# Attention stage of a macaron transformer layer: other steps for the scaling, the turns and the norms

## What is computed

```python
x = x + 0.5 * ffn(layernorm(x))
x = x + attn(layernorm(x), W_q, W_k, W_v, W_o)
x = x + 0.5 * ffn(layernorm(x))

def attn(x, W_q, W_k, W_v, W_o):          # 16 heads of 16
    q, k, v = (proj(W) for W in (W_q, W_k, W_v))
    scores = where(causal, q @ k.T / 4, -65504.0)
    return (softmax(scores) @ v).reshape(b, s, d) @ W_o.T
```

## Time and profile before

| | us |
|---|---|
| median of the three executions | 1705.95 |
| the profiled execution's own time | 1703.97 |
| its span, from first to last instruction | 1702.0 |
| TensorE busy | 1552.6 (91%) |
| VectorE, ScalarE, POOL busy | 886.3, 583.8, 590.4 |
| mean granted TensorE clock | 0.956 of full speed |

### The profile page before, as it was taken

How to read it: one execution, slowest core, us unless ns; L and a number is a source line. 1 busy time by engine, 2 the same in 40 slices (tenths; PEclk the granted TensorE clock), 3 DMA queues, 4 the chain that set the end, 5 groups by cost and what they waited for, 6 DMA issues and landing times. The chain is left out here.

```text
span 1702.0 us, 27697 instructions
## 1 busy us (share of the span) xinstructions
PE 1552.6 (91%) x8388; PEld 1138.9 (67%) x8389; DVE 886.3 (52%) x1844; ACT 583.8 (34%) x1110; POOL 590.4 (35%) x832
## 2 busy tenths in 40 slices
PE   6699999999999948989998999856999999999998
PEld 5688885666668835556665666535888766666787
DVE  5377633333336637666565666515775333333466
ACT  1322222222223224545554555514222222222232
POOL 3328812333330043453454353422377033333200
PEclk9999999999999978999998999867999999999999
DMA  7678832222237334344444344124196322222661
GB/s 235 212 268 286 288 122 76 88 87 87 87 127 239 101 109 106 87 113 110 129 123 112 97 118 125 61 75 161 62 341 225 103 88 87 88 87 86 196 209 50
DMA packets 176951, 231.88 MB, mean 136 GB/s; under 512 B 20162, under 2 KB 136386, under 8 KB 176850
## 3 DMA queue, kind: packets, MB, share of 16 engines
q1 hardware_dynamic: 157746, 173.94, 34.1%
q0 software_dynamic: 19104, 56.64, 9.4%
HBM read 117.47 MB, written 83.10 MB: 118 GB/s over the span
## 5 line engine op out<-in xcount | busy, mean ns | idle before, releaser
L943 PE MATMUL f_bank<-f_xparts,f_sw 128*128 128x512 f32 x1536 | 382.9, 399 | 23.4 <-DVE f_sw L881 21.0
L943 PEld LDWEIGHTS f_bank<-f_xparts,f_sw 128*128 128x128 f32 x1536 | 286.5, 193 | 80.9 <-issue 25.1
L1007 PE MATMUL f_bank<-f_ew,f_hid 128*128 x640 | 302.4, 595 | 3.5 <-ACT f_hid L654 3.5
L612 POOL DMA_INDIRECT outputs_by_choice<-f_xq,f_home x160 | 153.2, 957 | 424.8 <-DVE f_xq L904 402.1
L1571 DVE TENSOR_REDUCE at_mx<-at_ps 128x1 f32<-128x384 f32 (+3 forms) x352 | 212.6, 632 | 102.4 <-PE at_ps L1700 101.5
L1484 ACT ACTIVATE at_pT<-at_ps 128x512 f32<-128x512 f32 (+1 forms) x352 | 194.9, 560 | 87.1 <-PE at_ps L1716 77.0
L1401 POOL TENSOR_SCALAR_AFFINE_SELECT at_pT<-at_pT 128x128 f32<-128x128 f32 (+2 forms) x352 | 121.4, 347 | 255.9 <-ACT at_pT L1484 253.8
L894 DVE COPY f_hid<-f_bank 128x256 f32<-128x256 f32 x160 | 68.0, 425 | 242.5 <-PE f_bank L1015 242.5
L647 ACT ACTIVATE f_sil<-f_bank 128x256 f32<-128x256 f32 x160 | 61.5, 384 | 351.8 <-PE f_bank L1007 349.6
L580 POOL DMA_INDIRECT rows_by_slot<-f_xq,slot x128 | 141.2, 1103 | 110.3 <-DVEq L741 71.9
L1007 PEld LDWEIGHTS f_bank<-f_ew,f_hid 128*128 128x128 f32 x640 | 114.2, 189 | 97.4 <-issue 89.0
(11 more groups left out here) (160 smaller groups left out, 1968.7 us busy)
## 6 DMA issues: line engine op xcount, KB each, us to landing
f_ew<-in_L_ffn_routed_w_dram SPq DMA_DIRECT2D x96, 256.0 KB
f_rawx<-rows_by_slot SPq DMA_DIRECT2D x160, 128.0 KB, 1.9
f_ew<-outputs_by_choice SPq DMA_DIRECT2D x16, 1024.0 KB, 6.8
rows_by_slot<-zero POOLq DMA_DIRECT2D x10, 1024.0 KB, 18.5
f_rawx<-xn_turned SPq DMA_DIRECT2D x16, 512.0 KB
f_xq<-xn_rows POOLq DMA_DIRECT2D x32, 256.0 KB
at_qT<-at_hiT SPq DMA_DIRECT2D x64, 128.0 KB, 2.8
at_kT<-at_hiT SPq DMA_DIRECT2D x128, 64.0 KB, 2.7
```

The source lines that it names most:

```text
L612: nc.gpsimd.indirect_dma_start(dram.yk, bass.IndirectOffsetOnAxis(ap=home[:, i:i + 1], axis=0), yr[:, i % 4, :], None).then_inc(y_st[i % 4 ...
L943: ins = pe.matmul(ps[j % 2][:, :], sw12[:, wp, k, w, j * P:(j + 1) * P], xparts[:, u, xp, k, :], start=(i == 0), stop=(i == 3 * KD - 1))
L1007: ins = pe.matmul(rUp[r % 2][:, :], xsT[:, r % 2, k * P:(k + 1) * P], w12[:, bass.ds(e * (KD * 2 * RH) + k * 2 * RH, 2 * RH)], start=(k == ...
```

## The change

```diff
-    AT_TURN, AT_SEND, AT_FETCH, AT_SCALE, AT_OUT = 1, 2, 4, 7, {1: 9, 2: 5}
-    TURNS, TURNS2 = (3, 7), (7, 10)
-    ROUNDS = range(-4, TG + 5)
+    AT_TURN, AT_SEND, AT_FETCH, AT_OUT = 1, 2, 4, (2, 6)
+    TURNS, TURNS2 = (3, 7), (1, 6)
+    ROUNDS = range(-4, TG + 6)
@@ out_of
-        return (c, i % NG - 1) if AT_OUT.get(i % NG) == s and c is not None else None
+        return (c, AT_OUT.index(s)) if i % NG == 2 and s in AT_OUT and c is not None else None
@@ turn2_of, route_of
-        c = ours(i // NG - 1, 0, NB_)
-        return (c, TURNS2.index(s)) if i % NG == 3 and s in TURNS2 and c is not None else None
+        c = ours(i // NG - 2, 0, NB_)
+        return (c, TURNS2.index(s)) if i % NG == 1 and s in TURNS2 and c is not None else None
-        return ours(i // NG - 2, 0, NB_) if i % NG == 0 and s == 5 else None
+        return ours(i // NG - 2, 0, NB_) if i % NG == 1 and s == 9 else None
@@ SyncE
-                    if gr == 0 and s == 3 and 0 <= c - 2 < NB_:
+                    if gr == 1 and s == 10 and 0 <= c - 2 < NB_:
-                    if gr == 3 and s == 6 and 0 <= c - 1 < NB_:
+                    if gr == 3 and s == 10 and 0 <= c - 1 < NB_:
@@ GpSimd
-                    if gr == 3 and s == 5 and 1 <= c + 2 < NB_:
+                    if gr == 2 and s == 5 and 1 <= c + 2 < NB_:
                         deviation(0, c + 2, var1, eps1, rs1)
-                    if gr == 3 and 6 <= s < 6 + CT and 1 <= c + 2 < NB_:
+                    if gr == 2 and 6 <= s < 6 + CT and 1 <= c + 2 < NB_:
                         normalize1(c + 2, s - 6)
-                    if gr == 3 and 1 <= s < 1 + CT and 0 <= c - 1 < NB_:
-                        normalize2(c - 1, s - 1)
+                    if gr == 3 and 6 <= s < 6 + CT and 0 <= c - 1 < NB_ - 1:
+                        normalize2(c - 1, s - 6)
@@ VectorE
+            def normalize2(c):
+                dve.wait_ge(rs2, c + 1)
+                dve.wait_ge(xn2_st, 16 * c)
+                dve.wait_ge(*full("turn2", (c - 1, KD - 1)))
+                for t in range(CT):
+                    ins = v.tensor_scalar(xn2[:, t, :], xres[:, t, :], mv[:, 1, t, 0:1], rstd[:, 1, t:t + 1],
+                                          ALU.subtract, ALU.mult)
+                ins.then_inc(normed2, 1)
-                    if s == AT_SCALE and half_of(i) is not None:
-                        scale(*half_of(i))
-                    if gr == 3 and s in (3, 4) and 1 <= c + 2 < NB_:
+                    if s == 0 and half_of(i - 1) is not None:
+                        scale(*half_of(i - 1))
+                    if gr == 2 and s in (3, 4) and 1 <= c + 2 < NB_:
                         moments1(c + 2, s - 3)
+                    if gr == 3 and s == 0 and c == NB_:
+                        normalize2(c - 1)
```

More of the change, by code:

```diff
@@ L1360, in _ @@
                         load_x1(c + 3)
-                    if gr == 0 and s == 3 and 0 <= c - 2 < NB_:
-                        for k in range(KD):
-                            sp.wait_ge(*gone("turn2", (c - 2, k)))
-                        sp.dma_start(dram.xnT[:, :, bass.ds((c - 2) * CHUNK, CHUNK)], xnT2[:]).then_inc(xnT2_st, 16)
                     if s == AT_SEND and half_of(i) is not None:
@@ L1370, in _ @@
                         lay_out(proj_of(i, s))
-                    if gr == 3 and s == 6 and 0 <= c - 1 < NB_:
-                        sp.wait_ge(normed2, c)
-                        sp.dma_start(rows(dram.xn, c - 1), xn2[:]).then_inc(xn2_st, 16)
                     if s == AT_WEIGH + 2 and 0 <= i - 1 < TG:
                         take_out(i - 1)
+                    if gr == 1 and s == 10 and 0 <= c - 2 < NB_:
+                        for k in range(KD):
+                            sp.wait_ge(*gone("turn2", (c - 2, k)))
+                        sp.dma_start(dram.xnT[:, :, bass.ds((c - 2) * CHUNK, CHUNK)], xnT2[:]).then_inc(xnT2_st, 16)
                     if gr == 2 and s == 10 and 0 <= c - 1 < NB_:
@@ L1379, in _ @@
                         sp.dma_start(rows(dram.x2, c - 1), xres[:]).then_inc(x2_st, 16)
+                    if gr == 3 and s == 10 and 0 <= c - 1 < NB_:
+                        sp.wait_ge(normed2, c)
+                        sp.dma_start(rows(dram.xn, c - 1), xn2[:]).then_inc(xn2_st, 16)
                     if gr == 3 and s == 10 and 1 <= c < NB_:
```

## The result

| | before | after |
|---|---|---|
| median (lowest to highest), us | 1707.05 (1703.82 to 1710.88), 4 runs | 1680.95 (1678.15 to 1685.97), 4 runs |
| the profiled execution's own time | 1703.97 | 1678.15 |
| its span | 1702.0 | 1676.4 |
| TensorE busy | 1552.6 | 1545.0 |
| mean granted TensorE clock | 0.956 | 0.967 |

The ratio is 0.9849, 95% interval 0.9818 to 0.9881: faster by 26 us, where 42 were forecast. The time lies inside the range of 1650 to 1683, near its upper end. The steady stretch shrank by 17.6 us, and the prediction had said that the forecast falls if it shrinks by under 25.

A forecast was written before the change was run, and what follows sets the result against it. TensorE was taken to set the pace, losing time to waits and slow clock. Terms -11.2 - 13.8 - 11.6 + 3.0 + 6 x 0.2 - 5.0 - 3.2 - 1.0 = -41.6 us took 1703.97 to 1662 us; range 1650 to 1683.

The forecast's parts named there:

- rival B: Steady rounds: the transfer of the maxima becomes the wait, costing 27 us instead of 3; time 1686 us, chance 0.15.
- rival C: TensorE's slow clock does not come back, so 11.6 us are missing; time 1674 us, up to 1680, chance 0.17.
- Part 1: Product with the reciprocals and output projection, moved into the next round: TensorE's wait for the product goes, -11.2 us.
- Part 2: Output norm's tiles, turns and routing moved: waits for POOL's tiles go, -13.8 us; VectorE's fuller quarter 2 costs 6 x 0.2.
- Part 3: TensorE's clock in the steady stretch: slow clock costs 15.0 us; two drops of 1.7 us remain, so -11.6 us.
- Part 4: Maxima's transfer, with two 512 KB transfers issued about 2 us ahead: 0.5 us late six times, +3.0 us, ends 0 and +17.
- The rule that spoke against the change: SP's queue: descriptors are consumed in ring order, so the maxima stand behind the whole megabyte; about +12 us in part 4.
- Part 5: Drain: turns and routing run while the last reciprocals travel, -5.0 us; last norm on VectorE instead of POOL, -3.2 us.
- Part 6: Attention's start: the first input norm moves a round forward, -1.0 us, between 0 and 3.7.

## Why the prediction was right, and where not

It is right in its number, by a margin of 2 us to the range's end, and right about every wait it removed. But what happened is rival B, at a somewhat smaller price, and not the forecast: its own span of 1650 to 1672 was missed, and so was its own sign, 25 us off the steady stretch. That the number lies inside is luck. The upper end of 1683 was there for rival C, a clock that does not come back, and of the 15.0 us of slow clock only 2.5 stayed where C looked for them, without a wait; B itself stood at 1686, outside the range.

**Part 1** (product and projection) holds.'s 11.2 us are gone. The part had 10.8 us between reciprocal and product against 10.0 for the transfer; the row has 806.28 - 795.84 = 10.4 us and no wait. The part did not see that the product's old place, step 7, would have become a wait for reductions: that is shown by the run with both transfers behind and the product at step 7, 22 us slower.

**Part 2** holds: the 13.8 us are gone, quarter 2 has no wait for reductions (VectorE 11.65 us busy in 16.01; the part thought some 13 of 14.5), and the 0.2 us per period for it were not needed.

**Part 3** (clock) is right for what it counts. Full clock and hardly any idle time (312.7 of 314.9 us busy) are what the kernel with both transfers behind shows, where 314.4 was worked out; but the agreement is partly luck, since a full period is 52.85 us busy (rounds 13 to 16 above) and not 52.4, and the first of the six has one chunk's turns and routing less. The two drops left in the sum at 1.7 us are rounds 22 and 26: 17.24 against 16.0, 1.24 us each. The other 6 us of slow clock stand behind the waits of part 4 (14.17 us busy against 12.56 in rounds 20 and 24, 14.83 against 11.8 in round 28).

**Part 4** is the step that failed: "six times 0.5 us". It cost 13.8 us of waits and those 6 us of clock, 20 instead of 3, beyond the end of 17 that the part gave, since that end had no clock in it. Two things were wrong. The large transfers were said to go out about 2 us ahead. In rounds 8, 12 and 28 the load goes out 0.5 to 0.6 us ahead, because SP is busy with eleven transfers ahead of them (in round 12 until 807.42, 1.1 us after POOL's tiles are done). The part looked at the steps and not at SP's queue, whose nine lay-out transfers take 5.7 us to issue. In rounds 16, 20 and 24 the lead is 1.3, 1.7 and 1.9 us only because the load's own issue is drawn out to that length, with the maxima waiting behind it. And the load was priced at its bytes over 368 GB/s, 1.4 us; but in the changed kernel the small transfer's score comes no earlier than 4.7 us after the load's issue. With a lead of 2 us and a short issue the same number gives 2.7 us from the maxima's issue to the score, and the 0.5 us would have been about right: an estimate, which fits the rounds with the maxima on ScalarE's queue and a lead of 1.7 us, where the wait was 0.3 to 0.6.

The rule that spoke against the change (the Trainium skill, "DMA: Bandwidth & Descriptors", section "Queues, rings and completion order") named the right danger, and its +12 was nearer to the 20 than the forecast's +3. But the order within one queue is not needed for the lateness. The same section of the Trainium skill says that each engine goes round the rows that have work, packet by packet. By that, a small transfer on ScalarE's own queue should get its turn between the packets of a load on SP's. Here it was late all the same: issued 0.2 us behind, its first packet started 2.96 us after the issue, and the score came after 4.5 us. That section of the Trainium skill also has it that the write which reports a transfer as complete lands only after every earlier write of the same DMA engine, across its queues. That could account for the longer time from the last packet to the score, 1.28 us against about 0.5, but not for the late first packet; no run here tests it.

**Part 5.** The last norm: 3.51 us measured, 3.2 forecast; four tiles take 1.38 us on VectorE, less than 4 x 0.404. So the earlier trace rows held, and the roughly line rate that the Trainium skill gives GpSimd for one input ("GPSIMD Engine Reference", section "Engine selection") did not: 4.83 against 1.38 us. The drain gained 2.3 instead of 5.0. Rounds 31 and 32 gained 3.8 and 0.5, as the part has it, but rounds 29 and 30 grew from 11.03 to 11.74 and from 13.40 to 14.72: both turns and the routing of one chunk, 24 instructions that had been in the steady stretch (2297 there before, 2273 after), now fall behind it. The sum left this shift out.

**Part 6.** The start gained 4.0, not 1.0, of which 3.1 in round 3 (16.44 to 13.32 us, the clock 0.81 before and 1.00 after). In another run of a kernel with the same start that round took 14.81 at 0.88, so part of it is chance.

Summed for the steady stretch: -32.4 + 17 (part 4) - 1 (the two drops) - 1.2 (part 2) is -17.6, as measured.

## What to carry to other kernels

Price a transfer by when it lands, and read its place from the issuing queue's own timeline, not from the step it stands in: here eleven small transfers ahead of it pushed a megabyte right up against the one short transfer that TensorE waits for. A small transfer that is urgent is issued ahead of every large one near it; giving it a queue of its own freed it from the issue of the others here, but a load issued 0.2 us ahead still made it late. Here that is the version to use: both large transfers behind the maxima, 1653.85 to 1658.12 us, 3.1 to 3.3% under the kernel before and 1.4 to 1.6% under the changed one. And before calling a removed wait a gain, look for the next resource that gets late in the same round: the product's move was worth 22 us or nothing, depending on two transfers elsewhere.

## What was not expected of the hardware

- An 8 KB transfer took 2.0 us from issue to score with nothing large near, and 3.4 to 5.8 us (the changed kernel) behind a 512 KB load issued 0.5 to 1.9 us before it. Counted from the load's issue it was 4.7 to 6.3 us there, 4.5 to 5.0 us with the small transfer in another queue, and 3.8 to 5.0 us with only the load ahead.
- In a queue of its own its 18 packets took 0.2 to 0.7 us in all, but the first started 1.3 us after the issue with no load just ahead and 2.0 to 3.3 us after it with one issued 0.2 to 1.7 us before.
- SP's issue of the 512 KB load took 0.45 us in some rounds and 1.3 to 1.9 in others of the same kernel, right behind the issue of the `xn` transfer.
- TensorE's clock fell to the 1.2 GHz level (0.50 granted, two stretches of 1.5 us from 1003.00) with the engine never idle before, in some periods and not in others of the same kernel.
- Waits of 1.5 to 1.9 us left the clock at 1.00 (rounds 8, 12 and 16), those of 2.1 and 2.2 us did not (0.89 and 0.90); in the earlier trace rows one of 2.3 us in round 27 left it at 1.00. With the maxima on ScalarE's queue, waits of 1.7, 1.8 and 1.7 us (rounds 9, 13 and 28) had rounds at 0.90, 0.90 and 0.89. So the length of the wait alone does not tell.
